# Base product of 256 and 400 columns, lora product ahead of the values, heads' output copied by two engines, biases loaded per group

## What is computed

```
# 1 mixing: per sequence b a 32 x 32 matrix and a bias from the condition
h = gelu(gelu(cond @ W0 + b0) @ W1 + b1);  att = softmax(h @ W2 + b2)      # 8 weights
y = einsum('boi,bih->boh', einsum('bk,koi->boi', att, weight), x) + (att @ bias_k)[:, :, None]
# 2 attention: 32 query heads, 8 key/value heads of 16, rope, causal
x1 = x + attention(y, Wq, Wk, Wv) @ Wo
# 3 convolution over the 512 numbers, 9 taps, 4 groups of channels, plus a term of the condition
z = conv1d(x1, convw) + cond @ convc.T + fside
# 4 feed-forward: base product, and a router over 15 entries that weighs 8 rank-16 experts
w = top 8 of softmax(z @ routerW.T + routerb), mapped to 8 experts
out = x1 + z @ baseW.T + baseb + 2 * lora(z, A, B, w)
```

## Time and profile before

| | |
|---|---|
| profiled execution | 646.57 us, of it 644.6 in the span |
| runs | 641.46, 644.11, 644.9 us |
| TensorE busy | 608.1 us, 94% |
| VectorE busy | 477.1 us, 74% |
| ScalarE, GpSimd busy | 227.1 and 223.8 us, 35% each |
| mean granted TensorE clock | 0.974 of full |
| DMA | 71.23 MB, mean 110 GB/s |

### The profile page before, as it was taken

One profiled execution on the slowest core, in us unless ns is written; L12 is line 12 of the kernel. 1 busy time (PEld: TensorE's weight loads), 2 busy tenths in 40 slices (PEclk: granted clock), 3 DMA queues, 4 the chain that ended last, 5 costly groups with the idle time before them and its releaser, 6 DMA issues.

```text
span 644.6 us, 14143 instructions
## 1 busy us (share of the span) xinstructions
PE 608.1 (94%) x4928; PEld 504.9 (78%) x4928; DVE 477.1 (74%) x1201; ACT 227.1 (35%) x635; POOL 223.8 (35%) x181
## 2 busy tenths in 40 slices
PE   4977996999999999999999999999999999999885
PEld 3665775888888888888888888888888888888664
DVE  3556565788778787878877878787887787878743
ACT  4342332333333343334333334333433333433310
POOL 6253131443333333344333333334433333333310
PEclk9979797999999999999999999999999999999989
DMA  7746346444344455444344445544533344444430
GB/s 172 123 133 135 88 105 152 124 116 108 88 95 104 102 122 122 122 122 122 97 99 92 100 102 122 122 122 122 122 96 99 90 102 103 122 122 106 107 82 34
DMA packets 121446, 71.23 MB, mean 110 GB/s; under 512 B 48357, under 2 KB 103301, under 8 KB 121176
## 3 DMA queue, kind: packets, MB, share of 16 engines
q1 hardware_dynamic: 119952, 70.53, 44.9%
q10 hardware_dynamic: 1336, 0.24, 0.2%
q0 software_dynamic: 144, 0.28, 0.2%
HBM read 51.49 MB, written 19.53 MB: 110 GB/s over the span
## 4 chain that ended last, share of the span: by engine, by line
PE 86%; DMA 5%; DVE 5%; issue 2%; SPq 1%; ACT 1%; POOL 0%; ACTq 0%; DVEq 0%
PE ps L415 20%; PE ps L566 15%; PE ps L593 9%; PE ps L587 8%; PE ps L613 5%; PE ps L605 5%; PE ps L515 4%; PE ps L632 4%; PE ps L552 4%; PE ps L654 3%; PE ps L621 2%; PE ps L577 2%; DMA scratch<-x_dram 2%; PE ps L555 1%; PE ps L601 1%
## 5 line engine op out<-in xcount | busy, mean ns | idle before, releaser
L941 POOL TENSOR_TENSOR qk<-network,t 128x640 f32<-128x640 f32 x31 | 48.3, 1558 | 161.7 <-DVE t L1118 161.7
L415 PE MATMUL ps<-wqkv_hi,y_hi 128*128 128x512 f32 (+1 forms) x256 | 89.4, 349 | 8.5 <-POOL y_lo L933 7.0
L415 PE MATMUL ps<-wqkv_hi,y_lo 128*128 128x512 f32 (+1 forms) x256 | 88.7, 346 | 0.0
L415 PE MATMUL ps<-wqkv_lo,y_hi 128*128 128x512 f32 (+1 forms) x256 | 88.5, 346 | 0.0
L953 POOL TENSOR_TENSOR raw<-x1p,basebB 128x512 f32<-128x512 f32 x32 | 49.3, 1541 | 64.9 <-DVE x1p L1193 64.9
L745 ACT ACTIVATE raw<-ps 128x512 f32<-128x512 f32 x64 | 37.8, 595 | 76.0 <-PE ps L632 75.9
L415 PEld LDWEIGHTS ps<-wqkv_hi,y_hi 128*128 128x128 f32 x256 | 49.7, 194 | 17.1 <-DVE raw L1137 9.2
L964 DVE TENSOR_TENSOR oT_lo<-ps,oT_hi 128x256 fp32r<-128x256 f32 x64 | 24.2, 419 | 50.4 <-ACT oT_hi L745 50.4
L948 POOL TENSOR_TENSOR raw<-raw,zero 128x512 f32<-128x512 f32 x32 | 33.2, 1039 | 79.6 <-DVE raw L1182 79.6
L807 ACT ACTIVATE raw<-raw 128x512 f32<-128x512 f32 x64 | 40.4, 632 | 54.9 <-DVE raw L1137 54.9
L925 POOL TENSOR_TENSOR raw<-raw,rz 128x512 f32<-128x512 f32 x32 | 33.6, 1049 | 65.6 <-DVE rz L1147 65.6
(11 more groups left out here) (182 smaller groups left out, 1485.4 us busy)
## 6 DMA issues: line engine op xcount, KB each, us to landing
scratch<-x_dram SPq DMA_DIRECT2D x96, 256.0 KB, 4.8
x_dram<-x1p SPq DMA_DIRECT2D x32, 260.0 KB, 2.1
xm<-x SPq DMA_DIRECT2D x32, 256.0 KB, 3.8
xr<-x SPq DMA_DIRECT2D x32, 256.0 KB, 2.7
out<-raw SPq DMA_DIRECT2D x32, 256.0 KB, 2.1
v_dram<-vS SPq DMA_DIRECT2D x32, 64.0 KB
vB<-v_dram SPq DMA_DIRECT2D x128, 16.0 KB, 4.2
mixb<-mixb_dram SPq DMA_DIRECT2D x1, 1280.0 KB, 7.7
```

The source lines that it names most:

```text
L415: last = mm(dst, a, b, start=(n == 0), stop=(n == 3 * len(left) - 1))
L941: nc.gpsimd.tensor_tensor(qk[:, :], t1, t2[:, :], ALU.add).then_inc(qk_sb, 1)
```

## The change

The base product is split at column 256 instead of 384: bank 7 takes 256 base columns and the 144 others (400), bank 6 the first 256. The lora product is split 256 and 256. Its first product (high x high, bank 6) is issued ahead of the values, behind the values' waits; the two small products of line 648 go. Of the heads' output, ScalarE copies the half in bank 4 and VectorE the half in bank 7, each with a semaphore. The biases of groups 4 to 31 are loaded one group at a time, three steps ahead, and `next_y` waits for each. The transposes of baseW move to steps 0 and 1, baseW's load ahead of the values' first store, the copies of A, router and values of group 0 behind the first query copy, the Wo copies behind y's, and the loads of `mixw` for groups 4 to 31 to the end of SP's step 1.

```diff
-BASE6 = 3 * P
+BASE6 = 2 * P
 (SyncE)
             sp.dma_start(mixb[:, P:4 * P], mixb_row[P:4 * P].partition_broadcast(P)).then_inc(mixb_in, 16)
+            sp.dma_start(rawbase, baseW.rearrange("(p j) l -> p j l", j=PH)).then_inc(ld["base"], 16)
...
-            sp.dma_start(rawbase, baseW.rearrange("(p j) l -> p j l", j=PH)).then_inc(ld["base"], 16)
...
-            def late_bias(lo, hi):
-                sp.dma_start(mixb[:, lo * P:hi * P], mixb_row[lo * P:hi * P].partition_broadcast(P)).then_inc(mixb_in2, 16)
+            def load_bias(u):
+                sp.dma_start(mixb[:, bass.ds(u * P, P)],
+                             mixb_dram.rearrange("(g b) s -> g (b s)", b=NB)[bass.ds(u, 1), :].rearrange("a n -> (a n)")
+                             .partition_broadcast(P)).then_inc(mixb_in2, 16)
...
-                if peeled(t, 0):
+                if peeled(t, 1):
                     sp.wait_ge(mixw_out, 16)
                     load_mixw(sp, 4, G, mixw_in)
-                if peeled(t, 1):
-                    late_bias(4, 12)
-                if peeled(t, 2):
-                    late_bias(12, G)
+                if live(t + 3) and (not isinstance(t, int) or t > 0):
+                    load_bias(t + 3)
 (TensorE)
+            def lora_first(u):
                 pe.wait_ge(hwT_hi_sb, u + 1)
                 pe.wait_ge(hwT_lo_sb, u + 1)
+                if live(u + 2):
+                    values_ready(u + 2)
+                mm(ps[:, 6, 0:BASE6], hwT_hi[:, :], lora_hi[:, 0:BASE6], start=False, stop=False)
+            def lora(u):
                 terms = ((hwT_hi, lora_hi), (hwT_hi, lora_lo), (hwT_lo, lora_hi))
-                for n, (a, b) in enumerate(terms):
-                    last = mm(ps[:, 6, 0:BASE6], a[:, :], b[:, 0:BASE6], start=False, stop=(n == 2))
+                for n, (a, b) in enumerate(terms[1:]):
+                    last = mm(ps[:, 6, 0:BASE6], a[:, :], b[:, 0:BASE6], start=False, stop=(n == 1))
                 last.then_inc(ffn_ps, 1)
                 for n, (a, b) in enumerate(terms):
-                    last = mm(ps[:, 2, 0:P], a[:, :], b[:, BASE6:D], start=(n == 0), stop=(n == 2))
+                    last = mm(ps[:, 2, 0:D - BASE6], a[:, :], b[:, BASE6:D], start=(n == 0), stop=(n == 2))
 (project)
                 pe.wait_ge(oT_hi_sb, u + 1)
+                pe.wait_ge(oT_hi_dve, u + 1)
 (feed_forward)
-                    last = mm(ps[:, 7, 0:P + NAR], a, b[:, BASE6:D + NAR], start=(n == 0), stop=(n == len(terms) - 1))
+                    last = mm(ps[:, 7, 0:D - BASE6 + NAR], a, b[:, BASE6:D + NAR], start=(n == 0), stop=(n == len(terms) - 1))
 (values_ready: the waits that stood in values; values keeps them only where no lora goes ahead)
-                if not isinstance(t, int):
-                    mm(ps[0:S, 4, 0:2], convW[:, 0, :, :].rearrange("p j o -> p (j o)"), xc[:, 0, 0:2], start=True, stop=True)
 (steps)
-                if peeled(t, 1):
+                if peeled(t, 0):
                     pe.wait_ge(prep_sb, 1)
                     prepare_base((0, 1))
+                if peeled(t, 1):
+                    prepare_base((2, 3))
...
+                if live(t - 2) and not peeled(t, G):
+                    lora_first(t - 2)
                 if live(t):
                     values(t)
-                if peeled(t, 1):
-                    pe.wait_ge(oT_lo_sb, 2)
-                    prepare_base((2, 3))
 (ScalarE, at o_ps)
-                    for a in range(2):
-                        last = copy(heads(oT_hi, a), heads_ps(a))
-                    last.then_inc(oT_hi_sb, 1)
+                    copy(heads(oT_hi, 0), heads_ps(0)).then_inc(oT_hi_sb, 1)
 (ScalarE, steps: moved behind qT's copy)
+                if peeled(t, 0):
+                    prepare_ar()
+                    act.wait_ge(rope_t, 2)
+                    keep_values()
                 if live(t + 1):
                     next_y_hi(t + 1)
+                if peeled(t, 0):
+                    prepare_wo((0, 1))
 (VectorE)
-                v.tensor_tensor(x1b[:, 3, :], ps[:, 7, 0:P], x1b[:, 3, :], ALU.add).then_inc(last_sb, 1)
+                v.tensor_tensor(x1b[:, 2:4, :], ps[:, 7, 0:D - BASE6].rearrange("p (j n) -> p j n", j=2), x1b[:, 2:4, :], ALU.add).then_inc(last_sb, 1)
...
+                if not isinstance(u, int) or u > 3:
+                    dve.wait_ge(mixb_in2, 16 * (u - 3))
                 dve.wait_ge(y_ps, u + 1)
...
             def low_oT(t):
+                dve.wait_ge(o_ps, t + 1)
+                v.tensor_copy(heads(oT_hi, 1), heads_ps(1)).then_inc(oT_hi_dve, 1)
                 dve.wait_ge(oT_hi_sb, t + 1)
-                for a in range(2):
-                    last = minus(heads(oT_lo, a), heads_ps(a), heads(oT_hi, a))
-                last.then_inc(oT_lo_sb, 1)
+                minus(heads(oT_lo, 0), heads_ps(0), heads(oT_hi, 0))
+                dve.wait_ge(oT_hi_dve, t + 1)
+                minus(heads(oT_lo, 1), heads_ps(1), heads(oT_hi, 1)).then_inc(oT_lo_sb, 1)
```

More of the change, by code:

```diff
@@ L388, in steps @@
                     sp.dma_start(xr[:, :], group(x_g, t + 1)).then_inc(xr_in, 16)
-                if peeled(t, 0):
+                if peeled(t, 1):
                     sp.wait_ge(mixw_out, 16)
                     load_mixw(sp, 4, G, mixw_in)
-                if peeled(t, 1):
-                    late_bias(4, 12)
-                if peeled(t, 2):
-                    late_bias(12, G)
+                if live(t + 3) and (not isinstance(t, int) or t > 0):
+                    load_bias(t + 3)
             for t in range(0, 4):
                 steps(t)
-            with sp.Fori(4, G - 2) as t:
+            with sp.Fori(4, G - 3) as t:
                 steps(t)
-            for t in range(G - 2, G + 2):
+            for t in range(G - 3, G + 2):
                 steps(t)
@@ L635, in transpose_p, with values_ready @@
                         last.then_inc(pT_ps, 1)
[L637 to L648 removed]
+            def values_ready(t):
+                pe.wait_ge(vB_in, 16 * HK * (t + 1))
+                if peeled(t, 0):
+                    pe.wait_ge(base_lo_sb, 2)
+                if peeled(t, 1):
+                    pe.wait_ge(base_lo_sb, PH)
+                pe.wait_ge(pT_sb, 2 * t + 2)
+            def values(t):
+                if not live(t - 2):
+                    values_ready(t)
                 for b in range(NB):
@@ L850, in steps @@
                     act.wait_ge(ar_ps, t - 1)
-                    copy(arS[:, :], ps[:, 7, P:P + NAR]).then_inc(ar_sb, 1)
+                    copy(arS[:, :], ps[:, 7, D - BASE6:D - BASE6 + NAR]).then_inc(ar_sb, 1)
                 if live(t):
@@ L873, in steps @@
                     act.wait_ge(o_ps, t + 1)
-                    for a in range(2):
-                        last = copy(heads(oT_hi, a), heads_ps(a))
-                    last.then_inc(oT_hi_sb, 1)
-                if live(t + 1):
+                    copy(heads(oT_hi, 0), heads_ps(0)).then_inc(oT_hi_sb, 1)
+                if live(t + 1) and not peeled(t, -1):
                     act.wait_ge(rope_t, 2 * (t + 2))
                     keep_values()
-                if peeled(t, 1):
-                    prepare_base((2, 3))
             iterate(act, steps)
@@ L1179, in output @@
                 out3 = outS.rearrange("p (n j) -> p j n", j=PH)
-                v.tensor_tensor(out3[:, 0:3, :], ps[:, 6, 0:BASE6].rearrange("p (j n) -> p j n", j=3), x1b[:, 0:3, :], ALU.add)
+                v.tensor_tensor(out3[:, 0:2, :], ps[:, 6, 0:BASE6].rearrange("p (j n) -> p j n", j=2), x1b[:, 0:2, :], ALU.add)
                 dve.wait_ge(last_ps, t - 1)
-                v.tensor_tensor(out3[:, 3, :], ps[:, 2, 0:P], x1b[:, 3, :], ALU.add).then_inc(out_sb, 1)
+                v.tensor_tensor(out3[:, 2:4, :], ps[:, 2, 0:D - BASE6].rearrange("p (j n) -> p j n", j=2), x1b[:, 2:4, :], ALU.add).then_inc(out_sb, 1)
             def steps(t):
```

31 lines of the change are left out of this document (9 added, 22 removed).

## The result

The changed kernel takes 635.68 us (median of 12 runs, 634.11 to 638.52), the kernel before in the same series 642.44 (12 runs, 640.13 to 644.97). The ratio is 0.989 with a 95% interval of 0.9875 to 0.9913. The change makes the kernel faster by 6.8 us: little more than 1%, but clear of the noise. Forecast were 19.6 us and 624.5, and the range of 617 to 632 does not hold the result.

A forecast was written before the change was run, and what follows sets the result against it. TensorE, 94% busy, was taken to bound the kernel, with stalls and lower clock in the opening. Terms -8.2 - 7.7 - 1.5 + 0.3 - 3.6 + 1.1 = -19.6 took the median 644.11 to 624.5 us; range 617 to 632.

The forecast's parts named there:

- steady steps: Loop steps 3 to 30: cheaper lora products and split heads' copy gain 0.13 us a step, 3.6 us; bounds 9.8 and -2.8.
- step 2: Opening step 2: moved mixw and bias loads, mostly covered by the feed-forward, cost 0.3 us; bounds -0.5 and 2.
- step 0: Opening step 0: base transposes fill TensorE's gap and the clock may return earlier, gaining 1.5 us; bounds 0 and 3.
- Rival A: Steady steps: the extra change of array shape takes what the lora products save; 628.1 to 631 us; chance 0.18.
- Steps 1 and 3: Opening: late transposes and mixw leave step 1, gaining 7.7 us; per-group biases remove step 3's wait, gaining 8.2 us.
- Tail: Last two steps: later ar_ps and longer route2 delay hw, with nothing to hide them; net 1.1 us lost.
- B: Step 0: baseW's load delays the mixing weights' round trip, so mix(1) starts late; +6 us, 630.5 us; chance 0.13.
- C: Whole kernel gains more: full clock through step 0, steady steps gain 0.35 us each; 615.2 us; chance 0.11.

The follow-up runs named there:

- the second trace of before: The kernel before run once more with no edit, for a second profile; it took 641.63 us.
- the last kernel: Changed kernel, lora products all behind the values, mixw behind `vB`, ScalarE copying both halves in step 0, last two groups cut at 384: 621.45 us.
- the last two kernels: Changed kernel with no product ahead, mixw behind `vB`, ScalarE copying both halves in step 0: 622.21 us; with last two groups cut at 384: 621.45 us.

## Why the prediction was wrong

**The direction was right, the size was not.** Of a forecast 19.6 us, 6.8 came. Two steps of the working failed, the steady steps (5.9 us) and step 2 (3.8); one input, the profile of before, was 4.1 us too heavy; and in step 0 the clock fell as it had not been forecast.

**Steady steps: the term that failed.** "Ahead of the values ... I take 0.09 lost" was sized at 0.12 for the product's columns and up to 0.10 for its start, less the 0.15 of the small products (which makes 0.07). Measured: 0.32. With the 0.95 to the start of the small products before and the columns' 0.12 taken off, 1.42 - 0.95 - 0.12 = 0.35 is left for going from the small tiles to the full array and back, 0.29 if one takes the 1.01 of the kernel without the product ahead. Of it 1.11 - 0.95 = 0.16 lies in front of the product: in both kernels the copy of the probabilities, for which both wait, ends 0.87 after the convolution's start (332.75 + 0.59 above; before, against 345.03, the row below), and the small product starts 0.08 later, the full one 0.24 later. The other 0.31 - 0.12 = 0.19 lies behind it. The prediction charged one slow start of up to 0.10. With the run of two products ahead three parts show: 0.16 before the first product starts, 0.10 between it and the next (0.22 instead of 0.12), 0.08 on the way back. The run with two products ahead excludes a price per product, the one with none ahead gives 0.24 a step back. Over 27 steps the miss is 5.9 us; measured against the second trace of before it is 1.6 more. Rival A named exactly this mechanism and gave it 0.18; the place where the earlier trace rows spoke for it, 0.20 us without a releaser right behind the small tiles, was read and called "a fixed cost of the waits there". By the rule of the Trainium skill that the prediction quoted (TensorEngine Tiling (Array Packing), Key Properties: changing the mode drains the array), a turn costs something, and the trace agrees. The size, 0.2, the prediction had read from its own rows: with it the stretch would lose 0.29, and 0.32 was measured. It counted one turn a step before and two after; the scores, in tiles of 32x128 and 64x128, are a further one in both kernels, which changes nothing in the difference. Whether the time is the emptying itself or a weight load that can't be hidden beside the other shape, the runs don't separate.

```profile
345.31 0.59 ACT L745 ACTIVATE raw<-ps 128x512 f32<-128x512 f32 x1
```

The rest of this part held. Behind the values 1.30 for 1.28, with the bound where it was put: VectorE's copy ends at 335.08 and the projection starts at 335.19. A loop step behind a feed-forward of 400 and 256 columns takes no more for it: from the key transposes to the convolution 12.37 us, 12.41 before and 12.35 in its second trace.

**Step 2: the cover that was not there.** "most of that is covered. I cost it at 0.3" failed by 3.8 us. The argument set step 2's feed-forward (3.7 us) against step 1's wait (2.9), as if the loads would arrive as long after the step's start as in step 1. The feed-forward did put off the convolution, by 3.3 us: without its wait it would start 10.3 us after the step's start in step 1 of before (62.16 - 2.91 - 48.95) and 13.6 here (79.67 - 2.56 - 63.54). But the input came later too, by 2.9 us. In step 1 of before SP issued its loads 6.35 us after the step's start, and they landed within 5.3 us:

```profile
55.30 2.16 SPq L375 DMA_DIRECT2D scratch<-x_dram  x3
DMA to landing us min/median/max: 4.5/5.1/5.3
```

Here they were issued 7.61 us after it, behind an `xr` issue of 1.30 us, the four of mixw (2.49) and the bias (0.78), and took up to 7.5 to land. The landing time is not a matter of mixw: in step 2 the loads take 5.1 to 8.1 us in all kernels that have mixw elsewhere, the one before among them, and 6.1 to 8.0 in those that have it ahead. Why it is longer in step 2 than in step 1, no run shows. What mixw decides is the issue: 7.6 to 8.4 us after the step's start with it ahead, 4.1 with it behind `vB`, where step 2 took 19.22, close to the 19.00 of the earlier trace rows (5.4 in the last kernel, with a wait of 0.46). The lower clock after the stall (0.93) came on top. The profile of after shows the mildest case: in the four other kernels with mixw in this place the wait was 3.5 to 3.7 us and step 2 23.9 to 25.7. "Step 2 grows past 21 because of the mixw loads" was named as what would make the prediction wrong, and the upper bound, 2 us, was too low by half.

**Step 0: the clock.** 0.25 for 1.5, within the bounds. The transposes did fill the gap and the queries ran at full clock (37 to 40 us, clock 1.00), as argued. But the mix and the scores (30 to 33.5 us, clock 0.51) and the projection's first eight products (clock 0.51) stood at the lower one. The lower clock of the first cost nothing, since the queries began at 35.57 with it and at 35.55 without; that of the projection cost 1.5 us (3.48 instead of 1.94):

```profile
43.70 1.98 PE L573 MATMUL ps<-wo_hi,oT_hi 128*128 128x512 f32 x4 [1.24 <-DVE oT_hi L1174]
```

The same products take 1.17 us for four in the kernel without the product ahead, where step 0 took 17.13, although nothing in step 0 differs. Its mean clock is 1.00 there:

```profile
29.42:46.55 17.13, 13.35 (x116) 10.91 (x116) 11.24 (x24) 11.96 (x27) 10.38 (x7) 1.00 0.25 71
```

Of six kernels with this step 0, four took 17.1 us and two 18.9 and 19.45. What decides it, no run shows. Of the 2.3 us between the two traces here 0.7 is only where the step is cut: its first key transpose stands at 28.68 in the one and at 29.42 in the other, its queries at the same time. The 1.24 us in the row is partly new (0.90 in both traces of before): VectorE's half of the heads' copy stands behind its work for rope and the base there; with both halves on ScalarE in step 0 the last two kernels took 16.8.

**Steps 1 and 3: right.** Step 1 -8.45 for -7.7 (bounds 5 to 9.5; its own items, 9.5 - 0.9 - 0.5, make 8.1), step 3 -8.22 for -8.2, and the runs with one part alone confirm both causes. Nothing came late in step 3. No bias wait showed in any step.

**Tail: right, and the profiles hide it.** The two hw waits do come later by 0.83 and 0.70, as the sum of 0.84 each had it: line 669's transpose starts 26.72 us after the last key transposes, 25.89 before, with the wait grown from 0.21 to

```profile
616.73 0.33 PE L669 MATMUL ps<-cst,hw 128*128 128x128 f32 x1 [1.06 <-DVE hw L1114]
...
628.56 0.33 PE L669 MATMUL ps<-cst,hw 128*128 128x128 f32 x1 [1.98 <-DVE hw L1114]
```

From the last hw to the end it is 5.24 us instead of 6.59, and so the table has 0.2. But of these 1.35 us only 0.18 are work of the kernel: from that transpose to the issue of the last output it is 2.82 us (to 631.38), 3.00 before (638.01 to 641.01). The rest, 1.17, lies between this issue and the end of the span: 3.6 us in both traces of before, 2.4 in after and in the run with the biases alone, whose tail is the one of before. So it is not the change's; what makes it, no run shows. At one clock the tail of 400 and 256 columns costs 1.3 us more, 41.51 against 40.18 and 40.15 with the old cut, where 1.1 was forecast.

**The baseline.** The sum was made on one execution and carried over to the median of three, 644.11. Over 12 runs that median is 642.44, and the profiled execution was 4.1 above it. The lower clock of its tail (0.89) and 0.06 us a loop step are in its profile as if they were the kernel's own. The miss of 11.2 us in the time (635.68 for 624.5) is smaller than that of 12.8 in the difference (6.8 for 19.6) because of the baseline alone.

**The other rivals.** B is refuted: mix(1) started at 29.88 with 0.43 of wait for its weights, step 0 was not late. C did not occur (its 9.8 for the steady steps would have needed a free product ahead). The range failed because it left room for one miss and two came together. Step 2 (4.07) lay beyond its bound of 2; the loop's 0.09 us lost a step lies just inside its bound of 0.10, and the 0.15 against the second trace of before beyond it. A by its dearer price gave 630.1; with the 3.8 us of step 2 that is 633.9, already beyond the upper end of 632.

## What to carry to other kernels

Before putting a full-array product between two stretches of small tiles, count the changes of shape, not the columns: here a pair costs 0.3 us, two and a half times the product itself, and a second product in the same turn paid its columns alone. When a bulk load is moved from one step's queue to another's, follow it there, and compare two times: when the data is wanted, and when it arrives. Here both moved by about 3 us, and the wait came back one step later; it vanished only with the bulk load behind the last load that the step needs. An edit's worth shows best alone: the bias loads gave as much as the whole change, while the product ahead, the moved stall and the longer tail took back what the rest brought.

## What the runs showed of the hardware

- A turn from small tiles (96x32, 64x32) to the full array and back costs 0.29 to 0.35 us beyond the columns: about 0.16 before the full product starts, 0.10 between it and the next, 0.08 on the way back. A second product in the same turn costs its 0.11 alone.
- The same instructions in the opening ran at a mean granted clock of 1.00 or of 0.82: 17.1 or 19.45 us, of which 0.7 is an earlier start of the stretch. The tail did likewise, 41.4 at 0.97 and 43.6 at 0.89. That is 1.6 and 2.2 us, a quarter and a third of what the change brought.
- Four loads of mixing weights ahead on SP's queue, 2.5 to 4.4 us of issue, delayed the issue of the three loads behind them from 4.1 to between 7.6 and 8.4 us after the step's start. From issue to landing these took 6.3 to 7.5 us with the weights ahead and 5.7 to 7.4 with them behind.
- One broadcast of 64 KB a step ahead of them on the queue raised the median time from issue to landing of the convolution's loads from 4.8 to 5.7 us and of the `vB` loads from 4.2 to 4.9. The kernel was 7.8 us faster all the same, since the slack hid it.
